# Attention to experts: silu and a row split stand between ScalarE's early loads, the third last token tile is scattered whole, one register load for two tables

## What is computed

```
x = x + _L0_xattn_ref(_layernorm(x), ctx, ...)
x = x + _L0_ffn_ref(_layernorm(x), ...)
x = x + _L1_xattn_ref(_layernorm(x), ctx, mask)
x = x + _L1_ffn_ref(_layernorm(x), gate_kernel, gate_proj, up_proj, down_proj)

# _L1_ffn_ref
routing_weights, selected_experts = top_k(softmax(x2d @ gate_kernel), 8)
routing_weights = routing_weights / sum(routing_weights)
# rows sorted by expert, group_sizes rows for each
w0 = ragged_dot(sorted_inputs, gate_proj, group_sizes)     # 512 -> 192
w1 = ragged_dot(sorted_inputs, up_proj, group_sizes)
expert_out = ragged_dot(silu(w0) * w1, down_proj, group_sizes)   # 192 -> 512
# back to token order, weighted sum over the 8 experts
```

## Time and profile before

| | us |
|---|---|
| median of 3 runs | 1451.21 |
| lowest and highest | 1450.37, 1453.27 |
| span of the profiled execution | 1474.3 |

### The profile page before, as it was taken

One profiled execution on the slowest core, in us unless ns is written; L12 is line 12 of the kernel. 1 busy time (PEld: TensorE's weight loads), 2 busy tenths in 40 slices (PEclk: granted clock), 3 DMA queues, 4 the chain that ended last, 5 costly groups with the idle time before them and its releaser, 6 DMA issues.

```text
span 1474.3 us, 26984 instructions
## 1 busy us (share of the span) xinstructions
PE 1382.7 (94%) x7525; PEld 753.2 (51%) x7526; DVE 1022.1 (69%) x2467; ACT 505.4 (34%) x916; POOL 383.7 (26%) x313
## 2 busy tenths in 40 slices
PE   4799999999999999999999559999999999999997
PEld 3344444444444444455444236666666666666664
DVE  7879857976895656688776536666666666666664
ACT  1454543444435343422222113333333333333332
POOL 1000000000000000025556543444344344344443
PEclk9899999999999999999999769999999999999999
DMA  9975776766767778836748668889999888989785
GB/s 370 396 262 193 263 256 213 247 197 205 241 209 237 235 254 286 280 119 251 284 195 294 242 227 216 223 218 260 246 246 234 221 229 228 247 223 222 148 162 84
DMA packets 132696, 345.04 MB, mean 234 GB/s; under 512 B 15008, under 2 KB 19616, under 8 KB 125728
## 3 DMA queue, kind: packets, MB, share of 16 engines
q1 hardware_dynamic: 73488, 206.72, 41.6%
q0 software_dynamic: 34640, 85.74, 25.2%
q10 hardware_dynamic: 24512, 51.89, 10.8%
HBM read 192.68 MB, written 151.62 MB: 234 GB/s over the span
## 4 chain that ended last, share of the span: by engine, by line
PE 68%; DVE 16%; DMA 4%; issue 4%; ACT 3%; another core or an unknown queue 2%; ACTq 1%; SPq 1%; DVEq 0%; POOLq 0%
PE PS L1671 17%; PE PS L1673 17%; PE PS L1672 17%; PE PS L1933 5%; PE PS L1961 2%; PE PS L1962 2%; DMA split_experts<-HT 2%; DMA CST<-in_kv 1%; PE PS L1950 1%; DVE EX L1300 1%; PE PS L1951 1%; DVE EX L1306 1%; DVE nw L1027 1%; DMA X<-in_x 1%
## 5 line engine op out<-in xcount | busy, mean ns | idle before, releaser
L587 POOL DMA_INDIRECT out<-BIG,EX x159 | 247.2, 1555 | 354.9 <-issue 153.4
L1671 PE MATMUL PS<-BIG 128*128 (+1 forms) x795 | 269.5, 339 | 5.0 <-DVE BIG L1572 3.3
L1672 PE MATMUL PS<-BIG 128*128 (+1 forms) x795 | 269.5, 339 | 0.0
L1673 PE MATMUL PS<-BIG 128*128 (+1 forms) x795 | 269.5, 339 | 0.0
L1671 PE MATMUL PS<-HT,BIG 128*128 128x512 f16 (+1 forms) x512 | 194.1, 379 | 3.0 <-DVE HT L1101 1.4
L1672 PE MATMUL PS<-HT,BIG 128*128 128x512 f16 (+1 forms) x512 | 194.0, 379 | 0.0
L1673 PE MATMUL PS<-HT,BIG 128*128 128x512 f16 (+1 forms) x512 | 194.0, 379 | 0.0
L560 POOL DMA_INDIRECT rows_by_expert<-HT,POS x128 | 124.9, 976 | 122.6 <-DVE POS L1391 88.1
L1672 PE MATMUL PS<-BIG,EX 128*128 128x512 f16 (+1 forms) x376 | 143.8, 382 | 1.1 <-issue 1.1
L824 ACT ACTIVATE BIG<-PS 128x256 f16<-128x256 f32 x159 | 61.1, 384 | 243.3 <-PE PS L1951 229.0
L1673 PE MATMUL PS<-BIG,EX 128*128 128x512 f16 (+1 forms) x376 | 143.6, 382 | 0.4 <-issue 0.4
(11 more groups left out here) (264 smaller groups left out, 2218.0 us busy)
## 6 DMA issues: line engine op xcount, KB each, us to landing
BIG<-rows_by_expert ACTq DMA_DIRECT2D x159, 280.0 KB
HT<-in_experts SPq DMA_DIRECT2D x64, 640.0 KB, 4.6
BIG<-split_experts SPq DMA_DIRECT2D x32, 1152.0 KB
split_experts<-HT SPq DMA_DIRECT2D x96, 320.0 KB, 2.2
CST<-in_kv SPq DMA_DIRECT2D x64, 256.0 KB, 4.7
split_context<-RT SPq DMA_DIRECT2D x64, 256.0 KB, 4.5
BIG<-split_context SPq DMA_DIRECT2D x7, 2048.0 KB
rows_by_expert<-X SPq DMA_DIRECT2D x32, 280.0 KB
```

The lines of the kernel that those rows point to most:

```text
L587: pool.indirect_dma_start(a_out, bass.IndirectOffsetOnAxis(ap=IDY[:, u % V:u % V + 1], axis=0), yt[u % V], None, compute_op=ALU.add).then_ ...
L1671: mm(out, lh, rh, start=first, stop=False)
L1672: mm(out, lh, rl, start=False, stop=False)
L1673: return mm(out, ll, rh, start=False, stop=last_group)
```

## The change

- **ACT, ahead of the rounds.** One register read takes entries 0 to 5 of both tables (due and first row) instead of two reads of 8. Tiles 1 to 3 are loaded, then come silu(0) and tile_hi(1), in this order, and then the loads of tiles 4 and 5.
- **POOL.** Token tile 13 is scattered whole, all 8 columns, as tiles 10 to 12 are. Columns 0 to 3 of tiles 14 and 15 follow, then columns 4 to 7 of these two.
- **SP.** The pads of experts 0 to 7 are issued ahead of the loop instead of 0 to 3, and in the loop the pad of expert e+4 stands ahead of the weights of expert e.
- **Registers.** The due values of ACT and the start values of POOL go through `load_counts`, which takes the maximum of each with its lower bound into a second register. At a round's head ACT reads 12 due values, from the third on, instead of 16.

```diff
+def load_counts(eng, name, table, least, most):
+
+    loaded = [eng.alloc_register(f"{name}{i}") for i in range(table.shape[-1])]
+    held = [eng.alloc_register(f"{name}_held{i}") for i in range(table.shape[-1])]
+    eng.reg_load(loaded, table)
+    for to, of in zip(held, loaded):
+        eng.reg_alu(to, of, least, ALU.max)
+        eng.free_register(of)
+    return [eng.snap(x, donate=True, min_val=least, max_val=most) for x in held]
@@ sync
-            for e in range(WP):
+            for e in range(2 * WP):
                 pad_expert(e, 16 * e)
             sp.wait_ge(s_tab, 1)
-            with sp.Fori(1, NE // WP) as i:
+
+            def replace_expert(e, h):
+                wait_apart(sp, s_wl, e * 16, s_spassed)
+
+                done = sp.value_load(TCUM[0:1, bass.ds(e - WP, 1)], min_val=1, max_val=NTILE + 1)
+                sp.wait_ge(s_ed, done)
+                load_expert(e, h)
+
+            with sp.Fori(1, NE // WP - 1) as i:
                 for h in range(WP):
-                    pad_expert(i * WP + h, i * (16 * WP) + 16 * h)
-                    wait_apart(sp, s_wl, i * (16 * WP) + 16 * h, s_spassed)
-
-                    done = sp.value_load(TCUM[0:1, bass.ds(i * WP + (h - WP), 1)], min_val=1, max_val=NTILE + 1)
-                    sp.wait_ge(s_ed, done)
-                    load_expert(i * WP + h, h)
+                    pad_expert(i * WP + (h + WP), i * (16 * WP) + 16 * (h + WP))
+                    replace_expert(i * WP + h, h)
+            for h in range(WP):
+                replace_expert(NE - WP + h, h)
@@ gpsimd
-            for t in range(NT - 3, NT):
+            scatter_rows(NT - 3)
+            for t in range(NT - 2, NT):
                 scatter_rows(t, range(4))
             for w in range(4, TOPK):
-                for t in range(NT - 3, NT):
+                for t in range(NT - 2, NT):
                     scatter_rows(t, (w,))
...
-                start = load_ints(pool, "expert_start", TAB[0:1, 4, bass.ds(it * U, U)], 0, NTILE)
+                start = load_counts(pool, "expert_start", TAB[0:1, 4, bass.ds(it * U, U)], 0, NTILE)
...
-            start = load_ints(pool, "last_start", TAB[0:1, 4, bass.ds(LOOPS * U, REST)], 0, NTILE)
+            start = load_counts(pool, "last_start", TAB[0:1, 4, bass.ds(LOOPS * U, REST)], 0, NTILE)
@@ scalar
-                return load_ints(act, name, TAB[0:1, 1, bass.ds(t, count)], 16, 16 * NE)
+                return load_counts(act, name, TAB[0:1, 1, bass.ds(t, count)], 16, 16 * NE)
...
-            rows, due = rows_at("first_row", 0, U), experts_due("first_due", 0, U)
+            entries = [act.alloc_register(f"first{i}") for i in range(2 * LEAD)]
+            act.reg_load(entries, TAB[0:1, 1:4:2, 0:LEAD])
+            rows = [act.snap(x, donate=True, min_val=0, max_val=NE * CAP + (SPARES - 1) * P) for x in entries[LEAD:]]
+            due = [act.alloc_register(f"first_due{i}") for i in range(LEAD)]
+            for to, of in zip(due, entries):
+                act.reg_alu(to, of, 16, ALU.max)
+                act.free_register(of)
+            due = [act.snap(x, donate=True, min_val=16, max_val=16 * NE) for x in due]
             act.wait_ge(s_spare, 16)
-            for t in range(1, LEAD):
+
+            def load_early(t):
                 act.wait_ge(s_add[t], LANDED)
                 load_tile(t, 0, rows[t], due[t])
+
+            for t in range(1, 4):
+                load_early(t)
+            tile_silu(0, 0)
             tile_hi(1, 1, due[1])
-            tile_silu(0, 0)
+            for t in range(4, LEAD):
+                load_early(t)
             with act.Fori(0, LOOPS) as it:
-                rows, due = rows_at("tile_row", it * U + 4, U + 4), experts_due("tile_due", it * U, U + 8)
+                rows, due = rows_at("tile_row", it * U + 4, U + 4), experts_due("tile_due", it * U + 2, U + 4)
                 for u in range(U):
                     t = it * U + u
 
                     hidden_hi(t, u % 2)
-                    tile_hi(t + 2, u % 2, due[u + 2])
+                    tile_hi(t + 2, u % 2, due[u])
                     if u < TOPK - LEAD:
                         act.wait_ge(s_add[LEAD + u], LANDED)
-                    load_tile((u + LEAD) % U, t + (V + LEAD - U + 1), rows[u + LEAD - 4], due[u + LEAD])
+                    load_tile((u + LEAD) % U, t + (V + LEAD - U + 1), rows[u + LEAD - 4], due[u + LEAD - 2])
                     tile_silu(t + 1, (u + 1) % 2)
```

## The result

The changed kernel is **slower**: 1499.88 us (median of 4 runs, 1494.65 to 1506.21) against 1450.79 us for the kernel before on the same chip, a ratio of 1.0333, 95% interval 1.0302 to 1.0364. That is 49 us lost where 6 were forecast as won. The profiled execution took 1494.65 us, with a span of 1492.9.

The account below looks back on a forecast made before the run. PE's stream bounds the loop, so only the attention-experts seam, held by ACT's loads, could give much. Part 1's 6.5 and Parts 2 to 5's -0.3 make 6.2 us; 6 off the 1451.2 median gives 1445.2 us, range 1441 to 1450.5.

Parts of the forecast that it names:

- What bounds the kernel: PE is busy 580.6 of 585.0 us in the tile loop; only the seam between attention and experts can give much.
- 3.84 us for 12 matmuls of 384 columns: At the seam, PE's next gate and up product at 1.2 GHz, ending about 866.6 and covering ACT's high half if calm.
- Part 5: Loop's round heads: maxima added on ACT and POOL, ACT reads 12 due values instead of 16; 0.2 against 0.22 us.
- Net 0: Round heads: 0.22 us a head from four fewer entries balances 0.2 for the maxima; ends 2.3 us gained, 9.2 lost.
- Part 1: ACT's seam order: silu and tile 1's high half ahead of tiles 4 and 5's loads; 9.4 to 4.8 us, booked 6.5.
- what is late next: Tile 0's down product, needing ACT's high half behind two loads and two reads; 9.4 us stay if calm, 4.8 if slow.
- Part 2: POOL's seam order: tile 13's four moved scatters fit a 7.39 us gap, 16 scatters end 5.1 us earlier; no gain booked.
- Part 3: ACT's seam read of 12 in 0.79 us replaces two of 8; tiles 1 to 3 load up to 0.8 us earlier; worth 0.
- Part 4: SP's pads of experts 4 to 7 ahead of the loop: 0.86 MB, 2.3 us of DMA, covered; 0, -1 us in the range.
- The round heads eat it: Round heads: unmerged maxima lengthen ACT's head by 0.56 us, PE waits 18 times; 3.2 us slower, 1454.4; chance 0.07.
- Its turning point: Round heads: from about 0.35 us a head the gain is gone (0.35 less 0.05, times 18, is 5.4).
- The wait only moves: Seam: ACT's silu stays held until the DMA queues drain; gain 2 to 4 us, 1448; chance 0.17.

Follow-up runs that it names:

- e14: Changed kernel with table rows 170 words apart, so the loop's due read starts on a multiple of 16 bytes, on a 1451 us chip; ratio 0.9999.
- e4: Changed kernel with ACT's due read put back to 16 entries from entry 8i, still through the maxima; 1480.43 us, ratio 1.0014.
- e2: Changed kernel with table rows 170 words apart, so every loop read starts on a multiple of 16 bytes, on a 1479 us chip; 1478.06 us, 0.9989.
- e13: e7's kernel (read mended, ACT's new seam order, POOL's old order, two seam register reads) on a 1451 us chip; ratio 0.9998.
- e10: e7 with ACT's seam order of before too, so both orders of before with the read mended, on a 1451 us chip; ratio 0.9994.
- e9: e1's kernel plus unused register reads on POOL, which its trace doesn't show; one run, 1452.3 us beside 1450.96.
- e12: e1's kernel plus used register reads of 34 forms on POOL; no kernel time given, 8 entries at least 578 ns from word 0, 1857 from word 2.
- e1: Kernel before plus only the maxima of load_counts, 16 due entries from 8i; 1482.52 against 1478.97 us, ratio 1.0029.
- e5: e2 with POOL's scatter order of before; ratio 0.9984 against the kernel before at 1478.57 us.
- e7: e5 with two one-row register reads at the seam in place of one over two rows; ratio 0.998 against the kernel before at 1478.57 us.
- e6: e2 with ACT's seam order of before; ratio 0.9975 against the kernel before at 1478.57 us.
- e8: The changed kernel itself, run again on a 1479 us chip; 1523.61 against 1478.57 us, ratio 1.0304.
- e15: e6's kernel (read mended, ACT's old seam order, POOL's new order) on a 1451 us chip; ratio 1.0011.
- e17: Changed kernel, slow read kept, with hidden_hi moved to the end of the turn before; 1543.21 us, ratio 1.0624.
- e11: e2 with 128 already met waits on ACT near the kernel's start, on a 1451 us chip; ratio 0.999.
- e3: Changed kernel with all tables moved by two words, so the due read starts well and all others badly; 1535.87 us, ratio 1.0382.
- e16: e13 with hidden_hi ahead of the loads of tiles 4 and 5 and the reads, in the loop a turn earlier; 1468.36 against 1450.7 us, 1.0122.

## Why the prediction was wrong, point by point

**What bounds the kernel** was read rightly: PE's stream in the loop, with ACT's head at its very edge. The prediction even has the number that makes it dangerous, 0.15 us between ACT's chain and PE at a head. What was added there was paid at 19 heads, 41.2 us of waits. The prediction's 3.84 us for 12 matmuls of 384 columns is in the trace of before too, at a granted clock of 0.50: they start every 0.32 us, which is the 1.2 columns a ns of its "1.2 GHz", and take 3.84 us from 872.23 to 876.07. At a clock of 1.00 the same twelve take 1.95 us, from 900.81 to 902.76.

**Part 5, the failed step.** "A head reads 12 entries in 0.79 and 16 in 1.01 us" was used as a law of the count. Both reads start on a multiple of 16 bytes (8i+4 and 8i); the changed one starts at 8i+2, and so "Net 0" left out the one cost that came. I asked how many entries it has and not where it begins. What the runs showed in its place: 2.60 us in the chain at one head and 2.81 as a median, against 0.79. 2.02 us x 19 is 38 us, near the 41.2 us that PE waits at the heads. To be held against it, e14, the same kernel with the tables put right, its waits of PE and its stage:

```profile
PE PS L1702 <- DVE BIG L1603: 2.0, 3, 1.1
```

```profile
878.00:1435.00 557.00, 552.60 (x3433) 348.46 (x3431) 370.08 (x899) 179.28 (x448) 235.68 (x152) 1.00 0.88 214
```

The spans are 1492.9 and 1445.7, 47 us apart. e14's waits of PE at the heads are 2.4 us (1.42 in the first round, and the 2.0 above without the last tile's 1.08), so 41.2 - 2.4 = 39 us of the 47 are waits ahead of down products. Another 6 to 7 us go to the clock: in the four rounds that start at a granted clock of 0.57 to 0.64 PE is busy 31.1 to 31.5 us, in the others about 29.7. The last 2 us I can't place.

The trace of before had the sign of it. At its last head ACT reads 5 due entries from such a start, the longer of these two:

```profile
L104 ACTq TENSOR_LOAD <-EX x2: 290/1074/1857, 1439.2 to 1439.5; - x2
```

1857 ns for 5 entries, more than the 1012 for 16. (It was a weak sign: at that head a read of 7 entries from a good start took 1689 ns on DVE and 1037 on POOL.)

The maxima, the term that I did weigh, were sized well: 0.08 + 0.07 us of groups, 0.2 with the gaps. So was the gain of four entries, 0.22 against the 0.24 between the reads of e4 and e2.

**Part 1** had the mechanism right. The table load runs ahead of the wait (837.34, silu at 841.78), and PE's hole shrank to 1.30 us. The size was off: 6.5 us booked, 1.4 measured in the down product (e13 against e10), nothing beyond the interval in the time. Two terms were mis-sized. On the kind of chip of the timed runs the hole was 4.4 (e9), 4.7 (e12) and 6.0 us (e10) with the seam's orders of before, and not 10.54, which e1 shows again on a 1479 us chip (10.56); I had seen that my profile stood 23 us over the median and took 0.2 us off for it. And "what is late next" was named rightly, the high half behind two loads and two reads, but 2.2 us was set for the reads from a calm head, where they took 1.27 + 2.24.

**Part 2** was booked at nothing because POOL had 7.39 us of idle time. That cover was a property of the kind of chip. On the 1479 us chips it is there with the old order (7.48 us in e1, 7.41 in e5, 8.15 in e7), but the last scatter comes no earlier with the new one (864.2 to 866.6 in e2, e4, e6 and e8, 864.84 before, 859.7 forecast). Tile 14's first scatter, which the prediction had at 840.6 us with either order, starts there at 843.6 to 846.5 us with the new order against 841.1 to 842.6 with the old one, after a wait for DVE's places in both; why the places come later is not shown. On the 1451 us chips POOL idles 1.62 us ahead of tile 14 with the old order, and the four scatters put tile 0's load back: in the four combinations the transposes by 3.3 us (e14 against e13) and 5.8 us (e15 against e10, which has a later table as well). With ACT's old order that is a loss of about 3 us in the down product; with the new one it is hidden behind the high half.

**Part 3** priced the seam's read at 0.79 us. It took 3.49 us in the changed kernel:

```profile
L864 ACTq TENSOR_LOAD <-EX x1: 3490/3490/3490, 831.5 to 831.5; - x1
```

Its two rows of six are six pieces where two reads of eight are four. That it doesn't reach the end was right: e7 and e5 are alike.

**Part 4,** the pads, was not tried by itself. e10, which has of the change only the pads, the maxima and the shorter read, is at 0.9994 (0.9985 to 1.0004), so the three together are within some 2 us of nothing. (0.86 MB at the 341 GB/s of the earlier trace rows is 2.5 us and not 2.3, which changes nothing.)

**The rivals.** "The round heads eat it" was right in place, sign and multiplier, and wrong in cause and size: it had the unmerged maxima at 0.56 us, not the read at 2. Its turning point, 0.35 us a head, was passed more than five times over. The range had no room for it because its upper end was built from the dearest maxima and not from the dearest read; a bound from both sides for the read, 5 entries in 1.86 us, would have reached 1.86/5 x 12 = 4.5 us a head. "The wait only moves" is what the seam did on both chips.

**What stays open.** What holds ACT's silu on the 1479 us chips until 3 to 4 us after POOL's last scatter, and why those chips are 28 us slower, is not settled; the profile names no releaser. What decides whether the clock falls behind a wait is open too: it fell behind one of 2.57 us in e17 (1061.90) and not behind one of 3.31 us in the changed kernel (1366.74). No version beat the kernel before by more than 0.25%: the best are 0.9975 on a 1479 us chip (e6) and 0.999 on a 1451 us chip (e11), and e14, the same kernel as e11 without its waits, gave 0.9999 on the other one.

## What to carry to other kernels

A read of a table into registers had here a price by where it starts, not only by how many words it has: on ACT twelve words took 0.79 us from a multiple of 16 bytes and 2.81 from 8 bytes beyond it (medians of e2 and of the changed kernel), sixteen from such a multiple 1.04 (e4). So let it start on a multiple of 16 bytes and take its words in fours (on POOL five took 0.58 us and eight 0.58, seven 1.01, e12), and rather read four words too many than start two later. When a measured price is carried to a changed instruction, ask what else differs, the address and the strides too, and look for the odd case of it in the trace (here the rest of the loop). And idle time that is to cover a moved step must be there in the executions that are timed; a profile that stands 1.6% over the median, as it turned out on another kind of chip, is not evidence for that.

## What the runs showed of the hardware

- A register read from SBUF took the time of pieces of some 0.24 us, by my reading of e12 a piece being four words that start on a multiple of 16 bytes, or else one word: 16 words took at least 1.05 us or 3.6 to 4.2 us on POOL (e12). From a bad start ACT, PE's loader, DVE and POOL all read slowly (e3: medians of 2.9, 3.2, 2.1 and 2.6 us).
- One and the same read was not always equally long. On ACT twelve words took 0.79 us in the median and up to 1.6 from a good start (e2), 2.81 and up to 4.8 from a bad one (the changed kernel).
- A long wait of PE can cost more than itself. Behind waits of 3.08, 3.09, 3.19 and 3.74 us the granted clock was 0.57 to 0.64 over the next 4 us, and such a round took PE 1.4 to 1.8 us more of busy time. Behind waits of up to 2.53 us and one of 3.31 in the changed kernel, and of 0.74 to 1.50 us in e16, it stayed at 1.00; behind e16's first, of 2.83 us, it was 0.66.
- The same kernel took 1451 us on two chips and 1479 on two others, and the order in which engines became late at the seam was not the same on the two kinds.
